# A graph layer with its targets broadcast as bytes, its feature loads asked later, and its last groups reordered

## What is computed

```python
def ref(node_feats, edge_feats, chi_scalar, cutoffs, senders, receivers, ...):
    w_ij = silu(edge_feats @ rad_W1 + rad_b1) @ rad_W2 + rad_b2
    w_ij = w_ij + (silu(chi_scalar @ sph_W1 + sph_b1) @ sph_W2 + sph_b2)
    w_ij = w_ij.reshape(-1, NUM_HEADS, HEAD_DIM)
    q_i = (node_feats @ Wq).reshape(-1, NUM_HEADS, HEAD_DIM)[receivers]
    k_j = (node_feats @ Wk).reshape(-1, NUM_HEADS, HEAD_DIM)[senders]
    alpha = (q_i * w_ij * k_j).sum(axis=-1) / sqrt(HEAD_DIM)
    alpha = alpha * cutoffs[:, None]
    v_j = (node_feats @ Wv)[senders].reshape(-1, NUM_HEADS, HEAD_DIM)
    out = segment_sum(alpha[..., None] * v_j, receivers, num_segments=n_nodes) / 16
    return out.reshape(-1, NUM_HEADS * HEAD_DIM)
x = layernorm(x + ref(x, edge_attr_32, edge_attr_32_n2, edge_weight, src, dst, ...))
```

## Time and profile before

| | |
|---|---|
| median of three runs | 1997.65 us |
| the profiled execution's own time | 1996.43 us |
| its span, first to last instruction | 1995.1 us |
| PE busy | 1696.7 us (85%) |
| DVE busy | 1571.8 us (79%) |
| POOL busy | 1490.9 us (75%) |
| ACT busy | 575.1 us (29%) |

### The profile page before, as it was taken

One profiled execution on the slowest core, in us unless ns is written; L12 is line 12 of the kernel. 1 busy time (PEld: TensorE's weight loads), 2 busy tenths in 40 slices (PEclk: granted clock), 3 DMA queues, 4 the chain that ended last, 5 costly groups with the idle time before them and its releaser, 6 DMA issues. The chain is left out here.

```text
span 1995.1 us, 60316 instructions
## 1 busy us (share of the span) xinstructions
PE 1696.7 (85%) x14497; PEld 1242.1 (62%) x14497; DVE 1571.8 (79%) x4308; ACT 575.1 (29%) x1019; POOL 1490.9 (75%) x1575
## 2 busy tenths in 40 slices
PE   8788888888988888888888888888888888788896
PEld 7566566666666665666666666666666666566564
DVE  5588888888878888887887778777777787778696
ACT  5323233222322232222222222322222222223231
POOL 6777777777777777777777777777777777777774
PEclk9899999999999999998898889999989898999898
DMA  9855666566656656566565656656555565656553
GB/s 327 278 163 162 173 173 172 156 171 172 168 161 169 174 172 166 163 172 170 155 171 152 170 159 168 171 153 173 154 171 161 163 172 153 171 154 172 152 162 99
DMA packets 195480, 340.03 MB, mean 170 GB/s; under 512 B 81861, under 2 KB 107830, under 8 KB 195126
## 3 DMA queue, kind: packets, MB, share of 16 engines
q0 software_dynamic: 74784, 203.79, 37.6%
q1 hardware_dynamic: 112812, 126.13, 21.1%
q10 hardware_dynamic: 7530, 6.24, 1.2%
HBM read 321.03 MB, written 14.95 MB: 168 GB/s over the span
## 5 line engine op out<-in xcount | busy, mean ns | idle before, releaser
L599 POOL DMA_INDIRECT kvt<-kvtab,srcS x1542 | 1464.4, 950 | 474.4 <-issue 464.9
L695 ACT ACTIVATE hs<-bank,B 128x512 f32<-128x512 f32 x806 | 509.6, 683 | 1370.9 <-PE bank L614 959.5
L637 PE MATMUL bank<-W2r,hs 128*128 128x128 f32 x3224 | 502.0, 303 | 12.0 <-ACT hs L695 12.0
L849 DVE TENSOR_TENSOR t<-bank,kvt 128x512 f32<-128x512 f32 (+1 forms) x397 | 267.6, 674 | 295.8 <-DMA kvt<-kvtab,srcS 159.9
L637 PEld LDWEIGHTS bank<-W2r,hs 128*128 128x128 f32 x3224 | 425.6, 206 | 89.9 <-issue 69.2
L637 PE MATMUL bank<-W2s,hs 128*128 128x128 f32 x3224 | 458.7, 289 | 0.0
L637 PEld LDWEIGHTS bank<-W2s,hs 128*128 128x128 f32 x3224 | 427.6, 207 | 0.0
L652 PE MATMUL bank<-msg,oh 128*32 128x128 f32 x3224 | 179.0, 294 | 233.2 <-DVE accT L788 224.3
L652 PEld LDWEIGHTS bank<-msg,oh 128*32 128x32 f32 x3224 | 72.3, 110 | 423.8 <-issue 397.9
L866 DVE TENSOR_REDUCE bank<-t 128x32 f32<-128x512 f32 x403 | 280.1, 695 | 13.9
L864 DVE TENSOR_TENSOR t<-bank,t 128x512 f32<-128x512 f32 x403 | 274.1, 680 | 17.3 <-PE bank L627 15.0
(11 more groups left out here) (94 smaller groups left out, 667.8 us busy)
## 6 DMA issues: line engine op xcount, KB each, us to landing
eft<-in_ef SPq DMA_DIRECT2D x103, 512.0 KB, 8.2
kvA<-kvtab ACTq DMA_DIRECT2D x3200, 1.0 KB
kvS<-kvtab SPq DMA_DIRECT2D x2688, 1.0 KB
dbt<-dst SPq DMA_DIRECT2D x102, 384.0 KB, 7.0
kvt<-kvtab,srcS POOLq DMA_INDIRECT x1542
qwt<-qtab SPq DMA_DIRECT2D x403, 24.0 KB
kvtab<-kvt SPq DMA_DIRECT2D x24, 256.0 KB, 7.1
qtab<-qx SPq DMA_DIRECT2D x12, 384.0 KB, 6.5
```

Of the source, the lines that this page charges most:

```text
L599: pool.indirect_dma_start(kvt[:, (g - HX) % KS, t, :], None, kvtab, bass.IndirectOffsetOnAxis(ap=srcS[:, g * TG + t:g * TG + t + 1], axis= ...
L637: pe.matmul(WB[g % 2][:, t * D:(t + 1) * D], hs[:, g % HS, j, t * 128:(t + 1) * 128], w2[:, :], start=(j == 0 and t == 0), stop=False, ski ...
L695: act.activation(hs[:, g % HS, j, :], HB[i % 4][:, :], ACT.Silu, bias=B1[:, j:j + 1]).then_inc(m_si, 1)
L849: m = dve.tensor_tensor(t1[:, s, a:b, :], tiles(WB[s][:, :])[:, a:b, :], kv[:, :, 0:D], ALU.mult)
```

## The change

1. **Targets as low bytes.** `dst16` becomes `dst8`, an array of unsigned bytes, filled with the lowest byte of each target. The broadcast into `dbt` carries 96 rows of 2 KB (192 KB) where it carried 384 KB. `ot` compares these bytes with the lowest byte of the window's node, so `basep` is now made in two steps: an integer `nodep`, then a copy of its low bytes. The 4-byte targets land in `cutS` ahead of the cast; ACT's load of the rest of `cutS` waits for that cast (`s_db`).
2. **Features asked later.** `features(1)` goes to the queue inside the loop, behind the first query rows. `features(g//4 + 2)` is asked at the fourth group of every four, no longer at the first; `destinations` stays at the first.
3. **One preload for a next pass.** `features(1)` isn't asked again at the end. `features(0)` and `destinations(0)` are asked as soon as their buffers are free.
4. **The last groups.** For groups 401 and 402 `scat(g-3)` stands behind `l2(g)`. On DVE `collect(401)` moves behind the head sum of group 402, and two accumulates and `next_basei` move toward the end.

```diff
-    dst16 = nc.dram_tensor("dst16", [NG, G], i16, kind="Internal").ap()
+    dst8 = nc.dram_tensor("dst8", [NG, G], u8, kind="Internal").ap()
...
+        nodep = sb("nodep", [WP, NG], i32)
-        dbt = sb("dbt", [128, DS, 4, G], i16)
+        dbt = sb("dbt", [128, DS, 4, G], u8)
...
-            dst_words = dbt[:, :, :, :].rearrange("p b a g -> p (b a g)")
+            low_bytes = dbt[:, :, :, :].rearrange("p b a g -> p (b a g)")[:, 0:T]
-            db16 = dst_words[:, 0:T]
-            dbi = dst_words[:, T:3 * T].bitcast(i32)
+            dbi = cutS[:, :].bitcast(i32)
...
+            def low_byte(t):
+                return t[:, :].bitcast(u8).rearrange("p (g b) -> p g b", b=4)[:, :, 0]
...
-            dve.tensor_scalar(basep[:, :], base[0:WP, :], pidx, None, ALU.add).then_inc(s_win, 1)
+            link(dve.tensor_scalar(nodep[:, :], base[0:WP, :], pidx, None, ALU.add))
+            dve.tensor_copy(basep[:, :], low_byte(nodep)).then_inc(s_win, 1)
...
-                    dve.tensor_copy(db16[:, :], dbi[:, :]).then_inc(s_db, 1)
+                    dve.tensor_copy(low_bytes, low_byte(dbi)).then_inc(s_db, 1)
...
-            features(1, s_ef[1])
+            act.wait_ge(s_db, 1)
             act.dma_start(cutS[:, SE:T], cutT[:, SE:T]).then_inc(s_cut2, 16)
...
             query_rows(0)
+            features(1, m_ef[1])
             for g in range(NE):
                 if g + 1 < NE:
                     query_rows(g + 1)
-                if g % 4 == 0:
-                    q, b = g // 4 + 2, g // 4 + 1
-                    if q < NQP:
-                        if q >= ES:
-                            sp.wait_ge(m_l1, 8 * (q - ES + 1))
-                        features(q, m_ef[q % ES])
-                    if b < NQP:
-                        if b >= DS:
-                            sp.wait_ge(m_ot, 4 * (b - DS + 1))
-                        destinations(b, m_db[b % DS])
+                b, q = g // 4 + 1, g // 4 + 2
+                if g % 4 == 0 and b < NQP:
+                    if b >= DS:
+                        sp.wait_ge(m_ot, 4 * (b - DS + 1))
+                    destinations(b, m_db[b % DS])
+                if g % 4 == 3 and q < NQP:
+                    if q >= ES:
+                        sp.wait_ge(m_l1, 8 * (q - ES + 1))
+                    features(q, m_ef[q % ES])
                 sp_rows(g)
...
-            sp.wait_ge(m_l1, 2 * NE)
-            for q in range(2):
-                features(q, m_ef[q])
-            sp.wait_ge(m_ot, NE)
+            q, b = max(range(0, NQP, ES)), max(range(0, NQP, DS))
+            sp.wait_ge(m_l1, min(8 * (q + 1), 2 * NE))
+            features(0, m_ef[0])
+            sp.wait_ge(m_ot, min(4 * (b + 1), NE))
             destinations(0, m_db[0])
...
-                if g >= 3:
+                if 3 <= g < NE - 2:
                     scat(g - 3)
                 l2(g)
+                if g >= NE - 2:
+                    scat(g - 3)
                 if g >= 3:
                     fold_tiles(g - 3)
...
             scat(NE - 3)
+            fold_tiles(NE - 3)
             scat(NE - 2)
-            fold_tiles(NE - 3)
             fold_tiles(NE - 2)
...
-                dve.tensor_scalar(basep[:, :], basep[:, :], float(W), None, ALU.add).then_inc(m_up, 1)
+                dve.tensor_scalar(nodep[:, :], nodep[:, :], float(W), None, ALU.add).then_inc(m_up, 1)
+                dve.wait_ge(m_up, 3)
+                dve.tensor_copy(basep[:, :], low_byte(nodep)).then_inc(m_up, 1)
...
                 if g == NE - 1:
                     accumulate(NE - 4)
                     collect(NE - 3)
-                    collect(NE - 2)
...
                 if g == NE - 1:
-                    accumulate(NE - 2)
+                    collect(NE - 2)
...
+            accumulate(NE - 2)
             collect(NE - 1)
+            if (NE - 1) % 4:
+                next_basei()
             accumulate(NE - 1)
-            next_basei()
+            if (NE - 1) % 4 == 0:
+                next_basei()
```

More of the change, by code:

```diff
@@ L212, in gnn_program @@
             s_rows = sem("s_rows")
-            s_ef = [sem(f"s_ef{i}") for i in range(2)]
+            s_ef0 = sem("s_ef0")
             s_db0 = sem("s_db0")
@@ L357, in destinations @@
                 sp.dma_start(dbt[0:WP, b % DS, :, :].rearrange("p a g -> p (a g)"),
-                             dst16[4 * b:4 * b + 4, :].rearrange("(o a) g -> o (a g)", o=1)
+                             dst8[4 * b:4 * b + 4, :].rearrange("(o a) g -> o (a g)", o=1)
                              .broadcast_to([WP, 4 * G])).then_inc(signal, 16)
             def features_landed(q):
-                return 16 * sum(i % ES == q % ES for i in range(2, q + 1))
+                return 16 * sum(i % ES == q % ES for i in range(1, q + 1))
             def destinations_landed(b):
@@ L482, in gnn_program @@
                     destinations(0, s_db0)
-                    features(0, s_ef[0])
+                    features(0, s_ef0)
                 if b == min(9, NQB - 1):
@@ L606, in l1 @@
                 q = p // 2
-                if q < 2:
-                    pe.wait_ge(s_ef[q], 16)
+                if q == 0:
+                    pe.wait_ge(s_ef0, 16)
                 else:
```

15 lines of the change are left out of this document (7 added, 8 removed).

## The result

The changed kernel takes 2002.76 us (median of 8 runs, 2001.66 to 2004.21); the kernel before, run beside it, 1997.42 us (8 runs, 1995.63 to 1999.2). The ratio is 1.0028, with a 95% interval of 1.0019 to 1.0038: slower by 5.3 us. The forecast was 2001.0 us with a range from 1990.0 to 2006.5. The time lies inside that range. The forecast was "same", with its edge at 4 us; 5.3 us is beyond that edge, though the lower end of the interval (3.8 us) is not. The profiled execution of after took 2003.94 us, its span is 2002.6 us: 7.5 us more than before's 1995.1, so a little more than the medians show.

A forecast was written before the change was run, and what follows sets the result against it. POOL's start, its 1542 gathers and what follows the last were taken to bound the kernel. +8.6 us from the byte comparison and -5.2 at the end gave +3.4, from 1997.65 us a forecast of 2001.0, range 1990.0 to 2006.5.

The forecast's parts named there:

- What bounds the kernel: POOL's start, 1542 gathers at 1.25 us each and what follows the last set the time; POOL never waits for another engine.
- Start 0: Before the first gather: it waits for `kvtab`, which the change doesn't touch, so cost 0.
- `ot` at two per beat, 478 ns: VectorE's byte comparison: 212 ns fixed plus 266 ns stream, up from 344 ns in all.
- The rivals at 344 and 745 ns: `ot` at four per beat, unchanged hold: 1992.4 us, chance 0.08; at one per beat, no lock: 1989.7 to 1991.7, chance 0.12.
- Mean gather 956 ns: Expected sign on POOL: the mean gather rises from 950 to 956 ns through `ot`'s longer stream, +8.6 us.
- `ot`'s first use: POOL wants the shared way 0.13 us into a gather; an `ot` begun just ahead delays it: +8.6 us, +5.5 to +12.
- The second use: Rival: POOL needs the shared way again later in a gather and can't absorb 266 ns; up to +8.6, 2009.6 us, chance 0.08.
- The loads cost POOL nothing: Smaller broadcast and later feature requests: no gather slows for DMA load, the pace stays 1.25 us; cost 0.
- The ring's cover: POOL's wait for the ring, tightest at group 21: 1.85 us of cover, 0.8 left after VectorE's 0.13 a group; cost 0.
- The end, -5.2: After the last gather: late rows of group 401 and the layer's wait go, -5.0, `next_basei` -0.2; bounds -3.5 and -6.5.
- the two ways that made up the 0.33: Chance of slower: the main case exceeding +4 us, 0.72 x 0.35, plus the rival of POOL's second use, 0.08.
- 212 fixed ns: Part of a VectorE scalar step outside its stream, from line 337's 422 ns less 210 ns of stream, also used for `ot`.

The follow-up runs named there:

- e3: The changed kernel, with each comparison also summing its output into a column nobody reads; 3134.07 us, ratio 1.0077 to the kernel before.
- e1: The kernel before with the byte targets alone (byte table, broadcast, two-step window number); 3129.39 us, ratio 1.007 to the kernel before.
- e6: The kernel before with the byte targets alone, e1 run again; 3126.82 us, ratio 1.006 to the kernel before.
- e10: The changed kernel with every row gathered by POOL, no row fetches on SP and ACT; 2756.19 us.
- e2: The changed kernel without its byte part (16-bit nodes and comparison); 3093.63 us, ratio 0.9953 to the kernel before.
- e5: The changed kernel without its byte part, e2 run again; 3096.7 us, ratio 0.996 to the kernel before.
- e9: The kernel before with every row gathered by POOL, no row fetches on SP and ACT; 2750.69 us.
- e4: The kernel before, 16-bit targets, with `ot` written and read at every second element; 3130.83 us, ratio 1.0062 to the kernel before.

## Why the prediction was right or wrong

- **What bounds the kernel: right.** The stretch of gathers plus start plus end add up to the whole difference, and POOL waits for nobody.
- **Start 0: nearly.** +0.4 us; the gap ahead of the first gather, put down to issue, grew from 4.27 to 4.82 us. Why was not tested.
- **`ot` at two per beat, 478 ns: right.** 477 measured. The rivals at 344 and 745 ns fall. One per beat without a hold exists in the accumulating form (e3), but the sentence against that rival, "every other plain step here runs at two or more", does not hold for `oh`, which runs at one.
- **Mean gather 956 ns: right by luck in its size.** The step said +8.6 us for `ot`'s first use, with +5.5 as its lower bound. That use gave +5.2 (68 collisions of 119 ns in the mean, where starts spread evenly would have given 86 of 133). The second use, a rival at +8.6, is real at +1.6. Collisions with `oh`, which had no term, gave +3.7. With -0.4 from other steps that is +10.1 (+9.9 by the stretch). The failed sentence is "Starts of `ot` spread evenly over POOL's 1.25 us": they don't. The prediction saw that "a late `ot` shifts its neighbours", but gave that only a place in the range. One of its own signs of being wrong, "if the gather moves by another cause", was met in part. (It counted 50 `ot` ahead of slowed gathers in before; by the bounds of the table it is 45, and 2.9 us of delay where the formula gave 2.8.) That the longer `ot` moved `oh` is supported by the two traces, as said above, but no run has the longer `ot` alone at this pace: in e1, e6 and e10 `oh` slowed 15, 17 and 5 gathers, in e2 and e5 8 each, in e9 2, too few to decide. The moved loads aren't excluded.
- **The second use decides "from a slack under 0.2 us": right in kind, too dear in price.** I let it cost as much as the first. It costs only in the 0.12 us between the slack's end and the point from which POOL wins.
- **The loads cost POOL nothing: nothing speaks against it.** The page's mean rate fell from 170 to 159 GB/s and the median gather stayed at 946 ns; in e2 and e5 the slowed gathers (19 and 21) stand beside an `ot`, an `oh` or a step ahead of the loop, but for one of 0.02 us.
- **The ring's cover: right.** Near group 21 the 0.30 us gaps put down to a message are the issue gap itself.
- **The end, -5.2: right in direction, half the size.** The failed step is "asked some 15 to 20 us earlier, so this delay goes". The request did move: it stands 25.8 us ahead of the last gather's end, and stood 7.0 us ahead, so 18.8 us earlier. The delay went from group 401, but group 397 waited 2.48 us for its rows, TensorE's clock fell behind that, and VectorE carried a backlog to the end: the product of 401 started 2.8 us behind the last gather's start and not 0.7. So the product of 402 came 6.45 us behind it and not 4.66. The second failed step is the chain from it to the last accumulate, "4.7 us as before": it took 5.4, at a granted clock of 0.50 where before had 0.94. Those are 1.8 and 0.7 us, together the 2.5 between -5.2 and -2.8. That one wait set off the rest is read from the order of the rows; no run tests it.
- **The verdict.** +3.4 was forecast, +5.3 measured by the medians (+7.5 by the profiled executions). Of the 4.1 us between forecast and profiled execution 2.4 are the end, 1.3 the gathers and 0.4 the start. "Slower" had 0.33 and came, but not by either of the two ways that made up the 0.33. With `ot`'s first use, the start and the end as measured, the sum is 5.2 + 0.4 - 2.8 = +2.8, which is "same"; the second use at a fifth of its price and the collisions with `oh` made the rest.

What stays open: no run on the first chip has one half alone. By its trace the rest without the bytes should lie below before (the end's gain is its own, the hold is the bytes'), and e2 and e5 did lie 0.4 to 0.5% below; but on chips with another bound. It isn't shown that it beats before where before takes 1997 us.

## What to carry to other kernels

- Where GpSimd's gathers are the bound, a VectorE step costs by what it holds of the shared way, not by its busy time: a comparison of 477 ns slowed gathers, and one of 737 in another form slowed none. Fewer bytes in can be dearer: a 1-byte input fell from four elements a beat to two and doubled the hold.
- Two engines that run at a fixed beat beside each other do not meet at random. Count the collisions of *all* steps that can hold GpSimd, those at one element a beat with both inputs in SBUF too, since lengthening one step moves the others.
- A request moved ahead of the end may take its contention along. Look which rows land in the microseconds behind its new place before booking the gain.

## What the runs showed of the hardware

- GpSimd's gather needs the shared way twice. In these traces the first need is about 0.13 us into it, with no slack (slope -1.00 from x = 91 ns on). The second is felt when a comparison of 477 ns begins 347 to 473 ns into it; with one of 344 ns it was felt in none of 42 gathers.
- A comparison of 512 elements with a scalar from a pointer: 344 ns for 16 bit in and out, 477 for 8 bit in, 511 for 16 bit written at step 2, and 735 with an accumulator (medians; reading it out ends some 8 ns later). Of these only the last leaves GpSimd alone. The Trainium skill, "SBUF — State Buffer", section "SBUF: two separate sides", has the lock last for the whole step. The traces agree on its end: with POOL's need 0.13 us into a gather, 351 + 130 = 481 ns is where an `ot` of 477 lets go, and 216 + 130 = 346 where one of 344 did (in e4 it is 353 + 130 = 483 for one of 511, some 28 ns early). They differ on its beginning: an `ot` that began less than 91 ns ahead of a gather did not slow it, so the hold starts some 91 + 130 = 221 ns into the step, which is near the 212 fixed ns of the forecast.
- A two-input step at one element a beat held GpSimd when both inputs lay in SBUF: `oh`, 282 ns for 128 elements, slowed 18 gathers before and 63 after, and let go where it ends (1100 - 946 + 130 = 284 ns); `qx<-t,qx`, 0.68 us for 512, slowed four in each. With one input in PSUM, steps of the same shape and length slowed none.
- The same program took 1997 us in the first runs and 3106 to 3131 us on three numbered chips later, 1.55 to 1.57 times as long, with another engine as its bound. On one of them leaving out the row fetches saved 380 us. What makes it so, and whether it is the chip at all, was not found.
